# Older tiles ahead of new rows, and three weights transfers behind the fourth tile's rows, in the first rounds of an expert pipeline

## The chip, the cores and the metric

The kernel runs on one core of a Trainium2 chip. The metric is device time in microseconds of one execution; lower is better. TensorE does matmuls and transposes, VectorE, ScalarE and GpSimd work on what it leaves, and SyncE only issues transfers. Each engine takes its own instructions in order and waits for the others by semaphores.

## What is computed

All is float32, on four sequences of 256 tokens of width 256. A bidirectional decaying scan conditions x, an attention block follows (16 heads, 4 key heads), its output is added to x, a second scan conditions the sum, and a mixture of experts closes it. Only the last part matters here:

```python
logits = x @ gate_weight.T
probs = softmax(logits)
w, chosen = top_k(probs, 8)
w = w / w.sum(-1)
for e in range(64):
    gate, up = split(x @ gate_up_weights[e])
    final += combine[:, e] * ((silu(gate) * up) @ down_weights[e])
```

There are 1024 tokens of 256 values, 64 experts, 8 experts per token, and an inner width of 96.

## The kernel before, in words

Each engine has its own program (`block.sync`, `gpsimd`, `scalar`, `vector`, `tensor`), and the order of the work is the order in which these programs are written out.

**Sending.** After attention and routing GpSimd scatters each token's row to a slot of its expert in DRAM (`slot_rows`), eight scatters for each block of 128 tokens. The last two blocks send their 16 scatters at the very end, in an order by expert rank (L613), each pair counted on a semaphore `last_sent[j]`.

**Tiles, groups, rounds.** The expert stage takes tiles of 128 rows: 64 rows of one expert and 64 of the next. 96 tiles are processed (`SEQ`), of which the first 28 and the last 4 are the first rows of each pair of experts and the 64 between are further rows, whose experts are known only at run time. Tiles 0 to 3 are groups of one, later ones groups of two. Rounds are one group each for groups 0 to 3 and two groups (four tiles) each from then on: round 4 is tiles 4 to 7, round 5 tiles 8 to 11.

**A tile's steps.** SyncE loads the 128 rows (`load_rows`, L429, two transfers of 65 KB). Ten row buffers allow it to run ahead; from tile 10 on it waits for the `dest_ready` of the tile ten before. Tile d of the first four also waits for `last_sent[2d]` and `last_sent[2d+1]`. TensorE turns the rows (`turn_rows`, two transposes through L1387), VectorE copies them to SBUF (`copy_turned_rows`, L1306) and reads weight and destination of each row (`find_rows`, L1314). TensorE multiplies by gate and up weights (`gate_up`, L1685), ScalarE takes the silu (`silu`, L833), VectorE multiplies (`weigh`, L1323), TensorE turns the product (`turn_act`, L1387), ScalarE copies it (`copy_turned`), TensorE multiplies by the down weights (`down`, L1706), ScalarE copies the result out (`copy_out`) and GpSimd scatters it to `pair_rows` (L620).

**The software pipeline.** In iteration g TensorE's loop (L1714) does, in this order: dummy matmuls that keep its clock (`keep_clock(IDLE[g])`, L1712, only g = 0 to 3, with 5, 2, 3 and 2 of them), `turn_rows` of round g, `turn_act` of round g-2, `gate_up` of round g-1, `down` of round g-2. VectorE's loop (L1348) copies round g's turned rows and then weighs round g-1; in its first iterations it also makes a table of the further tiles (`tile_table`), whose columns TensorE turns at the end of iteration 5. ScalarE's loop (L882) does `copy_turned` of round g-2, `silu` of round g-1 and `copy_out` of round g-2.

**Weights.** 32 transfers of two experts each fill `wts`. SyncE issues the first 22. Ten are left to ScalarE's queue (`load_two`, L852), since their places are in use until the last rows are sent: three at the end of its iteration 2, behind a wait for `last_sent[7]`, one at the end of iterations 3 to 5, then two at a time. While the expert tiles run, no other transfers but rows, these weights and the outputs' scatters run.

Of the kernel before, what the change touches and what calls it, by code (L numbers as in the profile page):

```python
# [31 lines left out]
def adaln_attn_ffn(nc, x_t, side_t, cond, wu_t, wq_l, wk_l, wv_l, wq_t, wv_t, wgd_l, wo_l, gw_t, experts, out):  # L32
# [14 lines left out]
    TOPK = 8  # L47
# [22 lines left out]
    with ExitStack() as ctx:  # L70
# [7 lines left out]
        def sem(name):  # L78
            return ctx.enter_context(nc.semaphore(name))
# [16 lines left out]
        def tiny(name, shape):  # L96
# [184 lines left out]
        last_sent = [sem(f"last_sent{j}") for j in range(TOPK)]  # L281
# [3 lines left out]
        rows_ld = [sem(f"rows_ld{i}") for i in range(NROW)]  # L285
        gu_copied, dn_copied = sem("gu_copied"), sem("dn_copied")
        xt_done, xt_copied, gu_done, silu_done, act_ready, at_done, at_copied, dn_done, out_copied, dest_ready = (
            sem(n) for n in ("xt_done", "xt_copied", "gu_done", "silu_done", "act_ready", "at_done", "at_copied", "dn_done",
                             "out_copied", "dest_ready"))
# [51 lines left out]
        LAST = (NTB - 2, NTB - 1)  # L341
# [15 lines left out]
        ROUNDS = [[g] for g in range(TOPK // 2)] + [[g, g + 1] for g in range(TOPK // 2, NG, 2)]  # L357
        NR = len(ROUNDS)
        TABLE_AT = 5
        IDLE = (5, 2, 3, 2)  # L360
        AHEAD = 8

        late_two = free_scored + 7

        def two_kept(i):
            return wts[:, 2 * i * EW:2 * (i + 1) * EW].rearrange("p (e n) -> p e n", e=2)

        def two_experts(i):
            return experts[2 * i:2 * i + 2].rearrange("e p n -> p e n")
# [10 lines left out]
        def _(sp):  # L380
# [63 lines left out]
            for d in range(NDBL):  # L444
# [8 lines left out]
                else:  # L453
                    m = j - FIXED
                    if m == 0:
                        sp.wait_ge(rows_ready, 1)
                    if m % AHEAD == 0:
                        _, r16 = nc.values_load_multi_w_load_instructions(
                            t_rows[0:1, 2 * m:2 * (m + AHEAD)], engines=[SP_ENGINE], min_val=0, max_val=NE * CAP - R,
                            skip_runtime_bounds_check_because="each is 0 or an expert's base plus at most its row count less one tile")  # L460
                        for k in range(AHEAD):
                            base_of[m + k] = r16[2 * k:2 * k + 2]
# [163 lines left out]
        def _(act):  # L626
# [194 lines left out]
            def copy_turned(a):  # L821
                n = len(GROUPS[a])
                act.wait_ge(at_done, a + 1)
                if a >= 2:
                    act.wait_ge(dn_done, a - 1)
                copy(aT[a % 2][0:I, 0:n, :], ps[0:I, 4 + a % 2, 0:n * P].rearrange("p (k t) -> p k t", k=n)).then_inc(at_copied, 1)

            def silu(u):
                n = len(GROUPS[u])
                act.wait_ge(gu_done, u + 1)  # L830
                if u >= 1:
                    act.wait_ge(act_ready, u)
                nc.scalar.activation(sact[:, 0:n, :], ps[:, 2 + u % 2, 0:n * I2].rearrange("p (k i) -> p k i", k=n)[:, :, 0:I],  # L833
                                     ACT.Silu).then_inc(silu_done, 1)
# [14 lines left out]
            def load_two(i):  # L849
                if i == free_kept:  # L850
                    act.wait_ge(rows_ready, 1)
                nc.scalar.dma_start(two_kept(i), two_experts(i)).then_inc(wts_ld[2 * i // PER], 16)  # L852
# [3 lines left out]
            def copy_down(g):  # L856
                for d in GROUPS[g]:
# [3 lines left out]
                    if m == 0:  # L861
# [3 lines left out]
                        for i in range(3):  # L865
                            act.wait_ge(scattered[i], 16)
                    if m % AHEAD == 0:
                        _, o8 = nc.values_load_multi_w_load_instructions(
                            t_off[0:1, 1, m:m + AHEAD], engines=[ACT_ENGINE], min_val=0, max_val=(NE - 1) * EW,
                            skip_runtime_bounds_check_because="each is 0 or an expert's number times the width of its weights")  # L870
                        for k in range(AHEAD):
                            dn_off[m + k] = o8[k]
# [8 lines left out]
            next_two = late_two  # L881
            for g in range(NR + 2):  # L882
                us = ROUNDS[g - 1] if 1 <= g <= NR else []
                outs = ROUNDS[g - 2] if g >= 2 else []
                for a in outs:
                    copy_turned(a)
                for u in us:
                    silu(u)
                for a in outs:
                    copy_out(a)  # L890
                for u in us:
                    copy_down(u)
                if g == 2:
                    act.wait_ge(last_sent[TOPK - 1], 16 * len(LAST))
                    for i in range(next_two, next_two + 3):
                        load_two(i)
                    next_two += 3
                elif g > 2:
                    for i in range(next_two, min(next_two + len(outs), FIXED)):
                        load_two(i)  # L900
                        next_two += 1
# [6 lines left out]
        def _(dve):  # L908
# [234 lines left out]
            for u in range(NU):  # L1143
# [40 lines left out]
                if u == NU - 1:  # L1184
                    dve.wait_ge(out_done, NB)
                    xs = xT[:, :, b * T:(b + 1) * T]
                    link(V.tensor_tensor(xs, ps[:, 7, :].rearrange("p (m t) -> p m t", m=CC), xs, ALU.add))
                elif n == KV - 1:
                    dve.wait_ge(out_done, b + 1)
                    xs = xT[:, :, b * T:(b + 1) * T]  # L1190
# [156 lines left out]

            for g in range(NR + 1):  # L1348
                ins_ = ROUNDS[g] if g < NR else []
                for x in ins_:  # L1350
                    copy_turned_rows(x)
                    find_rows(x)
                us = ROUNDS[g - 1] if g else []
                for k in range(max(len(us), len(ins_))):
                    if k < len(us):
                        dve.wait_ge(dest_ready, us[k] + 1)
                        weigh(us[k])
                    if k < len(ins_):
                        copy_gate_up(ins_[k])
                if g == TABLE_AT:  # L1360
                    tile_table(5)
                if g == 0:
                    tile_table(0)
                    tile_table(1)
                elif g == 1:
                    tile_table(2)
                    tile_table(3)
                elif g == 2:
                    tile_table(4)
# [10 lines left out]
        def _(pe):  # L1380
# [253 lines left out]
            def turn_rows(g):  # L1634
                if g >= 2:
                    pe.wait_ge(xt_copied, g - 1)
                for k, d in enumerate(GROUPS[g]):
                    pe.wait_ge(rows_ld[d % NROW], 32 * (d // NROW + 1))
                    for cc in range(CC):
                        ins = T_(ps[:, g % 2, (k * CC + cc) * P:(k * CC + cc + 1) * P], xrow[d % NROW][:, cc * P:(cc + 1) * P])  # L1640
                ins.then_inc(xt_done, 1)
# [47 lines left out]
            def down(a):  # L1689
                pe.wait_ge(at_copied, a + 1)  # L1690
                if a >= 2:
                    pe.wait_ge(out_copied, a - 1)
                for k, d in enumerate(GROUPS[a]):
                    j = SEQ[d]
                    if j >= FIXED:
                        m = j - FIXED
                        pe.wait_ge(dn_copied, m + 1)
                    for h in range(2):
                        if j < FIXED:
                            w = (2 * j + h) * EW + CC * I2  # L1700
                            moving = wts[0:I, w:w + C]
                        elif h == 0:
                            moving = wts[0:I, bass.ds(off_of[m] + CC * I2, C)]
                        else:
                            moving = copy_dn[m % NCOPY][0:I, :]
                        ins = nc.tensor.matmul(ps[h * R:(h + 1) * R, 6 + a % 2, k * C:(k + 1) * C], aT[a % 2][0:I, k, h * R:(h + 1) * R], moving,  # L1706
                                               start=True, stop=True)
                ins.then_inc(dn_done, 1)
# [5 lines left out]
            for g in range(NR + 2):  # L1714
                outs = ROUNDS[g - 2] if g >= 2 else []
                if g < len(IDLE):
                    keep_clock(IDLE[g])
                for x in ROUNDS[g] if g < NR else []:
                    turn_rows(x)
                for a in outs:  # L1720
                    turn_act(a)
                for u in ROUNDS[g - 1] if 1 <= g <= NR else []:
                    gate_up(u)
                for a in outs:
                    down(a)
                if g == TABLE_AT:
                    pe.wait_ge(cols_ready, 1)
                    pe.wait_ge(at_copied, g - 1)
                    for k in range(3):
                        ins = T_(ps[:, 5, k * P:(k + 1) * P], t_cols[:, k:k + 1].to_broadcast([P, P]))  # L1730
                    ins.then_inc(cols_turned, 1)
# [60 lines left out]
```

## Time and profile before

| what | value |
|---|---|
| plain runs, median of 3 | 522.57 us |
| plain runs, lowest to highest | 521.33 to 523.16 us |
| the profiled execution, first to last instruction (its own time as far as it is known) | 576.6 us |
| mean granted TensorE clock in it | 0.947 |
| TensorE busy | 477.4 us (83%) |
| VectorE busy | 342.7 us (59%) |
| ScalarE busy | 305.9 us (53%) |
| GpSimd busy | 212.3 us (37%) |

The profiled execution is 54.0 us longer than the median of the plain runs. All times of rows below are its own, in microseconds from its first instruction. The iterations that the change touches lie between 331 and 360 us. PE is TensorE's matmuls, PEld its weight loads, DVE VectorE, ACT ScalarE, POOL GpSimd, SP SyncE; a q behind an engine is its sequencer, which issues transfers. A matmul is two records in the trace and a transpose one: `turn_rows` of a tile is x2, `gate_up` of a tile x8 and `down` x4.

### The profile page before, as it was taken

To read this page: it belongs to the slowest core of one execution; us is meant where nothing else is said; L and a number is where in the kernel's file an instruction comes from. 1 tells how busy PE (TensorE), PEld (TensorE's weight loads), DVE (VectorE), ACT (ScalarE), POOL (GpSimd) and SP (SyncE) were. 2 spreads that over 40 slices of the span, in tenths; PEclk is the share of its full clock that TensorE was granted. 3 is DMA by queue.
4 is the path that set the end of the run, shared out by engine and by line. 5 is a ranking of instruction groups with operands and counts; after the bars stand their busy time and mean duration, and the time that the engine had idled before them with its cause. 6 is when DMAs were issued, how large, how long until landed. Compare 5 with 4: busy or idle time off the path is not lost. (4 is left out here: it accounts for less than half of the span.)

```text
span 576.6 us, 10371 instructions
## 1 busy us (share of the span) xinstructions
PE 477.4 (83%) x3073; PEld 351.1 (61%) x3073; DVE 342.7 (59%) x1204; ACT 305.9 (53%) x854; POOL 212.3 (37%) x224
## 2 busy tenths in 40 slices
PE   4586999999899899999983766987988888888666
PEld 1366767877787678788653423765665666655322
DVE  4768496596685894795793564544355454553033
ACT  3456787885966887779864201333244343444200
POOL 0344110041114631025584642245444455445600
PEclk9799999999999999999996788999899899899879
DMA  8920862000301102002998739884444444330097
GB/s 283 411 70 19 167 131 74 1 1 0 76 1 54 69 30 73 2 1 74 345 404 291 278 107 298 227 288 129 111 115 115 113 128 127 107 95 13 19 363 304
DMA packets 47318, 79.49 MB, mean 138 GB/s; under 512 B 8266, under 2 KB 31127, under 8 KB 46880
## 3 DMA queue, kind: packets, MB, share of 16 engines
q1 hardware_dynamic: 36864, 55.34, 31.1%
q0 software_dynamic: 7680, 16.93, 8.2%
q10 hardware_dynamic: 2720, 6.55, 3.5%
q8 instruction: 26, 0.43, 0.3%
q14 instruction: 28, 0.23, 0.1%
HBM read 56.54 MB, written 26.44 MB: 144 GB/s over the span
## 5 line engine op out<-in xcount | busy, mean ns | idle before, releaser
L620 POOL DMA_INDIRECT pair_rows<-eout,dest x93 | 91.8, 987 | 99.5 <-ACT eout L634 78.2
L833 ACT ACTIVATE sact<-ps 128x192 f32<-128x192 f32 (+1 forms) x50 | 16.3, 325 | 122.7 <-remote 73.6
L1323 DVE SCALAR_TENSOR_TENSOR aact<-sact,wcol,ps 128x96 f32<-128x96 f32 x96 | 26.0, 311 | 92.6 <-issue 87.1
L1685 PE MATMUL ps<-wts,xg 128*64 (+1 forms) x512 | 71.5, 342 | 3.7 <-DVE copy_gu L1346 2.2
L691 ACT ACTIVATE lg<-lg,mneg 128x128 f32<-128x128 f32 (+1 forms) x128 | 56.4, 443 | 26.1 <-DVE mneg L1029 21.5
L1685 PEld LDWEIGHTS ps<-wts,xg 128*64 128x64 f32 x512 | 53.0, 143 | 16.5 <-issue 9.5
L541 POOL DMA_INDIRECT slot_rows<-rows,pair_slot x48 | 47.9, 998 | 37.2 <-issue 24.1
L1512 PE MATMUL ps<-oT,wo_sb 128*128 128x256 f32 x240 | 54.4, 380 | 0.0
L1706 PE MATMUL ps<-wts,aT 96*64 96x256 f32 (+1 forms) x256 | 49.8, 395 | 4.4 <-issue 3.4
L1512 PEld LDWEIGHTS ps<-oT,wo_sb 128*128 128x128 f32 x240 | 44.6, 190 | 6.2 <-ACT oT L634 0.7
L634 ACT ACTIVATE lg<-lg,rinv 128x128 f32<-128x128 f32 (+1 forms) x128 | 45.9, 448 | 2.5 <-issue 1.7
L1685 PE MATMUL ps<-copy_gu,xg 128*64 128x192 f32 x256 | 46.6, 337 | 0.0
L1029 DVE CUSTOM_DVE_ANT_0 lg<-ps,bm 128x128 f32<-128x128 f32 (+1 forms) x128 | 36.9, 352 | 11.3 <-PE ps L1468 9.5
L1306 DVE COPY xg<-ps 128x512 f32<-128x512 f32 (+1 forms) x50 | 33.2, 664 | 15.4 <-PE ps L1387 8.8
L1387 PE MATMUL ps<-ident,xrow 128*128 128x128 f32 x192 | 31.0, 294 | 12.1 <-DMA xrow<-slot_rows 6.8
L1387 PEld LDWEIGHTS ps<-ident,xrow 128*128 128x128 f32 x192 | 22.3, 149 | 28.6 <-issue 21.2
L1383 PE MATMUL ps<-hh,wqh 128*128 128x256 f32 x128 | 38.1, 298 | 1.6 <-DVE kl L988 1.6
L1706 PE MATMUL ps<-copy_dn,aT 96*64 96x256 f32 x128 | 33.9, 385 | 6.4 <-issue 6.4
L1706 PEld LDWEIGHTS ps<-wts,aT 96*64 96x64 f32 x256 | 27.3, 141 | 15.8 <-issue 4.8
L1384 PE MATMUL ps<-hl,wqh 128*128 128x256 f32 x128 | 36.7, 287 | 0.0
L1385 PE MATMUL ps<-hh,wql 128*128 128x256 f32 x128 | 36.7, 287 | 0.0
L501 POOL TENSOR_TENSOR eukv<-euk,vT 128x512 f32<-128x512 f32 x8 | 10.2, 1273 | 67.1 <-ACT euk L669 50.6
(237 smaller groups left out, 1184.4 us busy)
## 6 DMA issues: line engine op xcount, KB each, us to landing
wts<-in_experts_dram SPq DMA_DIRECT2D x22, 640.0 KB, 8.0
xrow<-slot_rows SPq DMA_DIRECT2D x192, 65.0 KB
pairs<-pair_rows SPq DMA_DIRECT2D x16, 512.0 KB, 11.2
wts<-in_experts_dram ACTq DMA_DIRECT2D x10, 640.0 KB, 6.1
slot_rows<-zero SPq DMA_DIRECT2D x1, 4160.0 KB, 24.2
wT<-in_wq_t_dram SPq DMA_DIRECT2D x4, 512.0 KB, 6.5
wq_raw<-in_wq_l_dram SPq DMA_DIRECT2D x1, 2048.0 KB, 14.6
wo_sb<-in_wo_l_dram SPq DMA_DIRECT2D x1, 2048.0 KB, 20.5
```

The lines of the kernel that those rows point to most:

```text
L541: nc.gpsimd.indirect_dma_start(out=slot_d, out_offset=bass.IndirectOffsetOnAxis(ap=pair_slot[:, t, k:k + 1], axis=0), in_=r[:, k, :], in_o ...
L620: nc.gpsimd.indirect_dma_start(out=pair_d, out_offset=bass.IndirectOffsetOnAxis(ap=dest[:, d:d + 1], axis=0), in_=out_rows(d), in_offset=N ...
L634: copy = lambda o_, i_, s=1.0: nc.scalar.activation(o_, i_, ACT.Copy, scale=s)
L691: ins = nc.scalar.activation(t, t, ACT.Exp, bias=mneg[:, u % 2, c:c + 1], scale=-1.0, accum_out=rsum[:, u % 2, c:c + 1])
L1029: ins = V.tensor_tensor_reduce(t, s, m, 1.0, FLT_BIG, ALU.add, ALU.min, mneg[:, u % 2, c:c + 1])
L1383: nc.tensor.matmul(o_, a[0], b_[0], start=start, stop=False)
L1384: nc.tensor.matmul(o_, a[0], b_[1], start=False, stop=False)
L1385: return nc.tensor.matmul(o_, a[1], b_[0], start=False, stop=stop)
L1387: T_ = lambda o_, i_, n=P: nc.tensor.transpose(o_, i_, ident[0:n, 0:n])
L1512: ins = nc.tensor.matmul(ps[:, 7, m * T:(m + 1) * T], wo_sb[:, n * G + h, m * P:(m + 1) * P], oT[:, h, :], start=(n == 0 and m == 0 and h ...
L1685: ins = nc.tensor.matmul(ps[h * R:(h + 1) * R, 2 + u % 2, k * I2:(k + 1) * I2], xg[u % len(xg)][:, k, cc, h * R:(h + 1) * R], moving, star ...
L1706: ins = nc.tensor.matmul(ps[h * R:(h + 1) * R, 6 + a % 2, k * C:(k + 1) * C], aT[a % 2][0:I, k, h * R:(h + 1) * R], moving, start=True, st ...
```

## The change

The set `OLD_FIRST` holds iterations 1 to 4. In these TensorE does `turn_act`, `gate_up` and `down` of the older rounds first and `turn_rows` of the new round last, and VectorE weighs the older round before it copies the new round's turned rows. The three transfers at the end of ScalarE's iteration 2 stand at the start of its iteration 3, ahead of `copy_turned`, and wait for the landing of tile 3's rows (`rows_ld[3]`) in place of the last pair of scatters. From iteration 5 on nothing is changed.

```diff
--- before.py
+++ after.py
@@ -358,6 +358,7 @@
         NR = len(ROUNDS)
         TABLE_AT = 5
         IDLE = (5, 2, 3, 2)
+        OLD_FIRST = range(1, TOPK // 2 + 1)
         AHEAD = 8
 
         late_two = free_scored + 7
@@ -882,6 +883,11 @@
             for g in range(NR + 2):
                 us = ROUNDS[g - 1] if 1 <= g <= NR else []
                 outs = ROUNDS[g - 2] if g >= 2 else []
+                if g == 3:
+                    act.wait_ge(rows_ld[3], 32)
+                    for i in range(next_two, next_two + 3):
+                        load_two(i)
+                    next_two += 3
                 for a in outs:
                     copy_turned(a)
                 for u in us:
@@ -890,12 +896,7 @@
                     copy_out(a)
                 for u in us:
                     copy_down(u)
-                if g == 2:
-                    act.wait_ge(last_sent[TOPK - 1], 16 * len(LAST))
-                    for i in range(next_two, next_two + 3):
-                        load_two(i)
-                    next_two += 3
-                elif g > 2:
+                if g > 2:
                     for i in range(next_two, min(next_two + len(outs), FIXED)):
                         load_two(i)
                         next_two += 1
@@ -1347,12 +1348,16 @@
 
             for g in range(NR + 1):
                 ins_ = ROUNDS[g] if g < NR else []
+                us = ROUNDS[g - 1] if g else []
+                if g in OLD_FIRST:
+                    for u in us:
+                        dve.wait_ge(dest_ready, u + 1)
+                        weigh(u)
                 for x in ins_:
                     copy_turned_rows(x)
                     find_rows(x)
-                us = ROUNDS[g - 1] if g else []
                 for k in range(max(len(us), len(ins_))):
-                    if k < len(us):
+                    if k < len(us) and g not in OLD_FIRST:
                         dve.wait_ge(dest_ready, us[k] + 1)
                         weigh(us[k])
                     if k < len(ins_):
@@ -1715,7 +1720,8 @@
                 outs = ROUNDS[g - 2] if g >= 2 else []
                 if g < len(IDLE):
                     keep_clock(IDLE[g])
-                for x in ROUNDS[g] if g < NR else []:
+                xs = ROUNDS[g] if g < NR else []
+                for x in xs if g not in OLD_FIRST else []:
                     turn_rows(x)
                 for a in outs:
                     turn_act(a)
@@ -1723,6 +1729,8 @@
                     gate_up(u)
                 for a in outs:
                     down(a)
+                for x in xs if g in OLD_FIRST else []:
+                    turn_rows(x)
                 if g == TABLE_AT:
                     pe.wait_ge(cols_ready, 1)
                     pe.wait_ge(at_copied, g - 1)
```

## Rows read from the trace of the kernel before

**Rows 1.** The page: busy time of each engine, and one kind of weights transfer.

```profile
PE 477.4 (83%) x3073; PEld 351.1 (61%) x3073; DVE 342.7 (59%) x1204; ACT 305.9 (53%) x854; POOL 212.3 (37%) x224
...
wts<-in_experts_dram ACTq DMA_DIRECT2D x10, 640.0 KB, 6.1
```

**Rows 2.** Stretches: us, busy per engine (instructions), granted clock, DMA share, GB/s.

```profile
342.00:347.50 5.50, 4.41 (x15) 2.25 (x16) 4.67 (x12) 1.16 (x4) 0.40 (x1) 0.50 0.47 94
347.50:354.00 6.50, 4.16 (x24) 2.21 (x22) 2.13 (x10) 0.91 (x3) 1.80 (x2) 0.89 0.97 340
354.00:360.00 6.00, 3.38 (x23) 2.07 (x24) 2.45 (x11) 0.91 (x3) 0.98 (x1) 0.93 1.09 298
...
403.00:500.00 97.00, 82.60 (x710) 58.85 (x711) 47.33 (x210) 38.17 (x112) 47.20 (x48) 0.96 0.42 116
```

**Rows 3.** TensorE's waits, 360 to 540 us: total us, times, longest.

```profile
PE ps L1706 <- issue: 9.8, 16, 1.1
...
PE ps L1387 <- DMA xrow<-slot_rows: 1.4, 1, 1.4
```

**Rows 4.** Timeline of TensorE: start, us, line, tiles, count, [idle before <-what ended it].

```profile
334.31 0.87 PE L1685 MATMUL ps<-wts,xg 128*64 128x192 f32 x8
...
339.05 0.41 PE L1387 MATMUL ps<-ident,xrow 128*128 128x128 f32 x2 [1.09 <-DMA xrow<-slot_rows]
...
343.47 1.55 PE L1685 MATMUL ps<-wts,xg 128*64 128x192 f32 x8
344.81 1.07 PE L1706 MATMUL ps<-wts,aT 96*64 96x256 f32 x4
345.81 3.49 PE L1712 MATMUL ps<-x2tm,ident 128*128 128x512 f32 x4
349.13 0.38 PE L1387 MATMUL ps<-ident,xrow 128*128 128x128 f32 x2
349.35 0.27 PE L1387 MATMUL ps<-ident,aact 128*96 128x128 f32 x1
...
354.05 0.44 PE L1387 MATMUL ps<-ident,xrow 128*128 128x128 f32 x2 [2.38 <-DMA xrow<-slot_rows]
354.32 0.27 PE L1387 MATMUL ps<-ident,aact 128*96 128x128 f32 x1
...
355.76 0.86 PE L1387 MATMUL ps<-ident,xrow 128*128 128x128 f32 x4
...
359.61 0.69 PE L1387 MATMUL ps<-ident,xrow 128*128 128x128 f32 x2 [1.37 <-DMA xrow<-slot_rows]
...
360.44 3.83 PE L1685 MATMUL ps<-wts,xg 128*64 128x192 f32 x32
364.10 0.60 PE L1706 MATMUL ps<-wts,aT 96*64 96x256 f32 x4
```

**Rows 5.** Timeline of SyncE's queue, three short stretches: loads of the expert rows.

```profile
336.64 0.47 SPq L429 DMA_DIRECT2D xrow<-slot_rows  x1
...
341.63 1.10 SPq L429 DMA_DIRECT2D xrow<-slot_rows  x2
...
351.24 1.87 SPq L429 DMA_DIRECT2D xrow<-slot_rows  x3
```

**Rows 6.** Timeline of ScalarE and of the transfers that it issues.

```profile
342.37 0.25 ACT L833 ACTIVATE sact<-ps 128x96 f32<-128x96 f32 x1 [20.15 <-remote]
...
345.93 1.50 ACTq L852 DMA_DIRECT2D wts<-in_experts_dram  x3
...
350.91 0.37 ACTq L852 DMA_DIRECT2D wts<-in_experts_dram  x1
...
355.88 0.42 ACTq L852 DMA_DIRECT2D wts<-in_experts_dram  x1
```

**Rows 7.** Timeline of VectorE: one copy of turned rows.

```profile
345.47 0.42 DVE L1306 COPY xg<-ps 128x256 f32<-128x256 f32 x1
```

**Rows 8.** The stretch 359 to 360 us; columns as in rows 2.

```profile
359.00:360.00 1.00, 0.39 (x2) 0.40 (x3) 0.00 (x0) 0.00 (x0) 0.00 (x0) 0.56 1.12 277
```

## The prediction, made before the changed kernel was run

> **What bounds the kernel now.** I began with the page. TensorE is busy for 477.4 of 576.6 us [rows 1], so it is the first suspect everywhere, but a mean over stages says little about thirty microseconds of one of them. The second view is the table of stretches [rows 2]. From 403 to 500 us TensorE is busy 82.6 of 97 us and the DMA engines 0.42: this is the steady pipeline, bound by TensorE's own stream. From 342 to 360 us, where the edited rounds run, it is busy only 4.4 of 5.5, 4.2 of 6.5 and 3.4 of 6 us, while the DMA share goes from 0.47 to 0.97 and then 1.09. So the first rounds are bound by something that arrives, and the rest by TensorE. The waits of TensorE from 360 us to the end of the experts confirm the second half: one wait of 1.4 us for rows among all of them (it spills over from 359.6) [rows 3]. A microsecond won or lost before round 5's matmuls should therefore go one to one into the time; one won anywhere earlier counts only if round 5 starts earlier.
>
> The third view is TensorE's timeline [rows 4]. Round 5 turns tiles 8 to 11 first; its last two transposes start at 359.61 after a wait of 1.37 us for the DMA of rows, and only then come turn_act(3), 32 records of gate_up at 360.44 and down(3) at 364.10. Round 4 has the same shape: the last transposes, tile 7's, start at 354.05 after 2.38 us of waiting for rows; the older steps run from 354.32 to 355.76. Round 3 does not wait for rows: tile 3 is turned at 349.13, right behind a keep_clock(2) that took from 345.81 on at the low clock.
>
> Why do rows come late? SyncE issues each tile's two loads back to back, 0.62 us apiece (three in 1.87 us) [rows 5]. Counting from tile 3 at 341.63, tile 11's two are the last two of the three that begin at 351.24, so they are issued by 353.11. Tile 2 shows what a load costs when little else moves: issue over at 336.64 + 0.47 = 337.11, rows used at 339.05 on ending a DMA wait, 1.94 us [rows 4, 5]. At that price tile 11 would be here at 353.11 + 1.94 = 355.05; it was used at 359.61. The 4.56 us between are contention: the three late weights transfers go out at 345.93 [rows 6], two more at 350.91 and 355.88, 640 KB each, five of the ten that ScalarE issues [rows 1], and the engines are full from 347.5 [rows 2].
>
> **The change, part by part.**
> The wait of the three weights transfers. Today it is for the last scatter, after which tile 3's loads are issued too (341.63). Tomorrow it is for tile 3's landing: 341.63 + 1.10 + 1.94 = 344.7 [rows 4, 5]. But ScalarE gets there only behind copy_out(0), at 345.93 [rows 6]. The new wait is thus met 1.2 us before it is reached: cost 0. It stands ahead of copy_turned(1) of round 3, as the old one did at the end of round 2; what is queued behind it on ScalarE is copy_turned(1), silu(2), copy_out(1) and the fourth weights transfer, and behind these TensorE's down(1) and, new, turn_rows(3), which now follows down(1). If ScalarE came early, this would be a real stall: bounds 0 and, if ScalarE were ready right after the last scatter at 341.63, 344.7 - 341.6 = 3.1 us. I take 0, since the row nearest is ScalarE's own. Nothing else on a DMA queue moves: the three issues, 1.50 us together, stay between copy_out(0) and copy_turned(1).
>
> Round 1. TensorE does gate_up(0) before turning tile 1, and VectorE does weigh(0) before it copies tile 1. In the trace silu(0) starts only at 342.37 although gate_up(0)'s records end at 335.2, an idle stretch put down to "remote" [rows 4, 6]. If that lag stays, VectorE's copy of tile 1 moves behind weigh(0), to about 343.1, and takes 0.42 us as another 128x256 copy does [rows 7]: 343.5, against gate_up(1) at 343.47 now: no gain, no loss. The two table steps of this round follow that copy in either version, now later; they have until the table's transposes, behind down(3) at 364.10.
>
> Round 2. down(0) no longer stands behind tile 2's transposes, which had arrived anyway. 0.
>
> Round 3. The older steps of tile 1 and 2 run ahead of tile 3's transposes. Both follow keep_clock(2), which holds TensorE until 349.13 [rows 4]. Tile 3 has been there since 344.7, so nothing is waited for by going either way: the fourth weights transfer goes out some 0.3 to 0.5 us later, since tile 2's transposes now precede keep_clock(2). It is queued behind the first three, which at the 340 GB/s of the stretch [rows 2], 0.34 MB a microsecond, need 1.92 / 0.34 = 5.6 us from about 347.5, to 353: its own issue at 350.91 is not what sets its start. 0.
>
> Round 4. Here the order acts. turn_act(2), gate_up(3) and down(2), 354.32 to 355.76 = 1.44 us, leave the place behind tile 7's arrival and fill the 2.38 us gap before it [rows 4]. Then tile 7 is turned at the same 354.05 and TensorE goes on to round 5 1.44 us sooner, at 354.3. Round 5, outside the edited range, still turns tiles 8 to 11 first, and tile 11 comes at 359.61. The 1.44 us are added to the gaps that end there. Late next: tile 11. Gain 0 unless tile 11 moves. Its loads hang on SyncE's stream, which in this stretch waits for neither TensorE nor VectorE (0.62 us after 0.62 us), and on the same five transfers. The fifth now goes out about 2 us sooner (down(2) ends near 353.4 instead of 355.8), but it is served behind the fourth; at 0.34 MB a microsecond four transfers take until about 355 alone and near 358 with the rows between them, so its earlier issue brings between 0 and -1 us of contention to tile 11. I take 0.
>
> **Sum.** 0 + 0 + 0 + 0 - 0: the profiled execution would stay at 576.6 us. That execution is 54.0 us above the plain median of 522.57 (521.33 to 523.16), so its microseconds are not to be taken at face value one by one; I carry the difference, zero, over to the plain runs: 522.6. A measurement can tell about 0.3%, 1.6 us, from no change.
>
> **Rivals.**
> Faster: TensorE's order is what delays the rows' users, and in plain runs tile 11 isn't late. For it: those runs are 54 us shorter, so the contention may be less. With tile 11 in time, the 1.44 us of round 4 and as much of round 3 (the same steps for the tile before, from 349.35 on, at the same clock) come out of the path: 2.9 us, 519.7. The most that can go is the whole contention on tile 11, 4.56 us: 518.0. Against it: even with free DMA engines SyncE's stream holds tile 11 until 355.05, after round 4's work at 354.3.
>
> Slower, one mechanism: the clock. Between 354.3 and 359.6 TensorE keeps only transposes once the 1.44 us of matmuls have moved out. Now it is granted 0.56 of its clock at 359 to 360 us [rows 8], the lower level, 1.2 GHz, after it was nearly idle, and part of gate_up(4, 5) runs at it: 3.66 us from 360.44 to 364.10. If the clock is at the low level for the whole of round 5's older steps, a tile's gate_up takes 344.81 - 343.47 = 1.34 us [rows 4], four of them 5.4, 1.7 more than now, and down(3) 1.00 instead of 0.6: together +2.2 us, 524.8. It decides if the clock falls before 359 and isn't back before 364. The Trainium skill, "TensorE: Matmul & The Clock Gate", section "HAM oscillation — how this bites in real kernels", says that work in short bursts between waits for DMA is throttled again at each wait, which speaks against emptying this stretch; the trace agrees, with 0.56 at 359. By that page alone the result would be this rival's.
>
> The second way to a loss has the same size: in a plain run without the 7 us lag ScalarE is at the transfers right after the last scatter, and the new wait holds them, and all behind them, up to 3.1 us; DMA engines that stood at 0.47 then stay idle longer and tile 11 comes later by part of it. I count it in the range and in the slower chance.
>
> The change may also do nothing that it says: the new wait is met before it is reached. That is part of my forecast.
>
> **Chances.** No change 0.40; the faster rival 0.34, since gaps on three engines shrink in these rounds and only one arrival keeps them from counting; clock 0.12 and held-back transfers 0.14, slower 0.26 in all. The range runs from a little beyond the faster rival, 519.0, to a little beyond the slower one, 525.2.
>
> **What would show it.** After: tile 7's transposes still end a wait for rows near 354, now with turn_act(2), gate_up(3) and down(2) before them; tile 11's still end a wait near 359.6 and the gap before is longer by 1.4 us; ScalarE's three transfers go out within 0.5 us of 345.9; copy_turned(1) isn't held. Wrong if round 5's gate_up starts over 1.5 us earlier (or later) relative to the last scatter, if ScalarE sits before the transfers waiting for rows, or if gate_up(4, 5) takes 5 us.

## The result, and the profile after

The changed kernel is slower: 528.24 us median (524.33 to 531.02, 17 runs) against 523.89 us (520.45 to 528.09, 17 runs) of the kernel before on the same chips. The ratio is 1.0070, with a 95% interval of 1.0044 to 1.0095, so the 0.7% (3.7 us) is clear of noise; the two medians lie 4.35 us apart, and I go by the ratio. I had forecast no change.

The first reading is a correction of my own reference. The changed kernel was profiled in an execution of 527.56 us, span 525.8. The profile on which the prediction rests had a span of 576.6. A second profile of the unchanged kernel (run `base_again`) has a span of 524.3, in an execution of 526.11 us, the slowest of its twelve (the fastest took 521.50), so it too is no average execution. The stretches of that second profile, with the columns of rows 2, at the same distances from the last scatter of rows as rows 2:

```profile
331.50:337.00 5.50, 1.43 (x4) 0.36 (x2) 2.44 (x9) 0.00 (x0) 1.00 (x1) 0.94 0.85 271
337.00:343.50 6.50, 5.58 (x28) 3.64 (x30) 2.21 (x10) 1.13 (x4) 0.99 (x1) 0.53 1.02 287
343.50:349.50 6.00, 5.40 (x57) 3.88 (x53) 3.76 (x18) 1.57 (x6) 0.98 (x1) 1.00 0.97 296
...
392.50:489.50 97.00, 96.61 (x970) 74.34 (x969) 64.81 (x270) 59.71 (x164) 65.62 (x67) 1.00 0.45 131
```

and of the changed kernel:

```profile
331.00:336.50 5.50, 3.15 (x18) 1.33 (x17) 2.77 (x10) 0.64 (x3) 1.00 (x1) 0.94 0.59 143
336.50:343.00 6.50, 4.67 (x22) 2.39 (x20) 1.99 (x9) 1.07 (x4) 1.98 (x2) 0.50 1.06 352
343.00:349.00 6.00, 2.70 (x8) 1.16 (x8) 2.13 (x10) 0.00 (x0) 0.00 (x0) 0.50 1.07 331
...
392.00:489.00 97.00, 96.61 (x974) 74.67 (x972) 65.83 (x275) 60.34 (x165) 64.02 (x65) 1.00 0.47 132
```

Set beside [rows 2], the last line of each matters most. In the steady part TensorE is busy 96.6 of 97 us in both, not 82.6. The first profile was of an execution in which much else waited, and the wait structure that I read from it (ScalarE idle until 342.37, [rows 6]) was its own. In the other lines the two kernels part: in the third stretch TensorE is busy 5.40 of 6 us before and 2.70 after, at a granted clock of 1.00 before and 0.50 after, with the DMA engines full in both (0.97, 1.07). The changed kernel is still waiting for rows there.

The pages, sections 1 and 5: the changed kernel's line of busy times, and its wait of TensorE for rows over the whole span.

```profile
PE 459.3 (87%) x3073; PEld 344.4 (65%) x3073; DVE 345.9 (66%) x1204; ACT 310.1 (59%) x854; POOL 213.3 (41%) x224
...
L1392 PE MATMUL ps<-ident,xrow 128*128 128x128 f32 x192 | 30.3, 295 | 5.8 <-DMA xrow<-slot_rows 5.8
```

To compare stages I count from the start of the last of the scatters: 328.63 in `base_again`, 328.14 in the changed kernel. (Over all profiles it lies between 325.37 and 331.06, and for one kernel run twice, `order_only` and `order_again`, at 325.77 and 327.97, so a part of what executions differ by comes before the stage that the change touches.) In the timelines the columns are start, busy time, engine, line, operation and, in brackets, the idle time before it and what ended it; ACTq is ScalarE's issuing of DMAs. GpSimd's timeline of the kernel before, second profile:

```profile
328.63 0.96 POOL L613 DMA_INDIRECT slot_rows<-rows,pair_slot  x1 [0.31 <-issue]
```

its ScalarE's:

```profile
325.60 0.25 ACT L833 ACTIVATE sact<-ps 128x96 f32<-128x96 f32 x1 [14.44 <-PE ps L1685]
...
331.07 0.38 ACT L634 ACTIVATE eout_first<-ps 128x256 f32<-128x256 f32 x1 [0.18 <-PE ps L1706]
331.12 1.49 ACTq L852 DMA_DIRECT2D wts<-in_experts_dram  x3
338.84 0.27 ACT L634 ACTIVATE aT<-ps 96x128 f32<-96x128 f32 x1 [7.38 <-PE ps L1387]
...
341.19 0.38 ACTq L852 DMA_DIRECT2D wts<-in_experts_dram  x1
...
344.53 0.37 ACTq L852 DMA_DIRECT2D wts<-in_experts_dram  x1
```

and its TensorE's:

```profile
324.68 0.87 PE L1685 MATMUL ps<-wts,xg 128*64 128x192 f32 x8
...
337.93 0.66 PE L1387 MATMUL ps<-ident,xrow 128*128 128x128 f32 x2 [4.99 <-DMA xrow<-slot_rows]
...
345.88 0.44 PE L1387 MATMUL ps<-ident,xrow 128*128 128x128 f32 x2 [0.60 <-DMA xrow<-slot_rows]
...
346.36 2.82 PE L1685 MATMUL ps<-wts,xg 128*64 128x192 f32 x32
...
352.51 0.95 PE L1387 MATMUL ps<-ident,xrow 128*128 128x128 f32 x4 [1.99 <-DMA xrow<-slot_rows]
...
354.17 4.10 PE L1685 MATMUL ps<-wts,xg 128*64 128x192 f32 x32
```

The same three of the changed kernel, GpSimd's:

```profile
328.14 0.96 POOL L614 DMA_INDIRECT slot_rows<-rows,pair_slot  x1 [0.30 <-issue]
```

ScalarE's:

```profile
330.15 0.39 ACT L635 ACTIVATE eout_first<-ps 128x256 f32<-128x256 f32 x1 [0.18 <-PE ps L1711]
333.38 1.70 ACTq L853 DMA_DIRECT2D wts<-in_experts_dram  x3
335.13 0.27 ACT L635 ACTIVATE aT<-ps 96x128 f32<-96x128 f32 x1 [4.59 <-issue]
...
336.28 0.39 ACTq L853 DMA_DIRECT2D wts<-in_experts_dram  x1
...
339.82 0.38 ACTq L853 DMA_DIRECT2D wts<-in_experts_dram  x1
```

TensorE's:

```profile
336.17 0.69 PE L1392 MATMUL ps<-ident,xrow 128*128 128x128 f32 x2
...
343.00 0.69 PE L1392 MATMUL ps<-ident,xrow 128*128 128x128 f32 x2 [0.93 <-DMA xrow<-slot_rows]
344.82 0.66 PE L1392 MATMUL ps<-ident,xrow 128*128 128x128 f32 x2 [1.13 <-DMA xrow<-slot_rows]
...
349.36 0.69 PE L1392 MATMUL ps<-ident,xrow 128*128 128x128 f32 x2 [0.43 <-DMA xrow<-slot_rows]
...
350.19 4.14 PE L1690 MATMUL ps<-wts,xg 128*64 128x192 f32 x32
...
357.01 2.82 PE L1690 MATMUL ps<-wts,xg 128*64 128x192 f32 x32
```

What is to be seen, in microseconds after that scatter:

| | before (`base_again`) | changed |
|---|---|---|
| ScalarE's first three weights transfers | 2.5 | 5.2 |
| copy_turned(1) | 10.2 | 7.0 |
| fourth transfer | 12.6 | 8.1 |
| fifth transfer | 15.9 | 11.7 |
| tile 3 turned | 9.3 | 8.0 |
| tile 11 turned (last transposes of round 5) | 17.3 | 21.2 |
| duration of gate_up(4, 5), 32 records | 2.82 us | 4.14 us |
| duration of gate_up(6, 7), 32 records | 4.10 us | 2.82 us |

ScalarE is done with copy_out(0) at 330.15 + 0.39 = 330.54 and stands idle until 333.38: the new wait holds it for 2.8 us, and copy_turned(1) behind it has 4.59 us of idle time before it. Tile 3 does come earlier. Then both later weights transfers go out over 4 us sooner than before, and tile 11 is turned 4.0 us later and still ends a wait for its rows, whose loads were issued at the same distance in both. By the start of round 7 (tile 16) the difference is down to 2.1 us, 33.4 against 31.3: in round 6 it is the kernel before that waits 1.99 us for rows (at 352.51) and then runs its 32 records of gate_up at the low clock.

### The profile page after: what moved, and what is told of

The parts are those of the page before. It is cut to its first block and busy times, and to the rows that moved or that the text cites. A ratio compares the mean times of both kernels' runs of the same rounds, so it can differ in the third digit from the quotient of the medians.

```text
span 525.8 us, 10369 instructions
## 1 busy us (share of the span) xinstructions
PE 459.3 (87%) x3073; PEld 344.4 (65%) x3073; DVE 345.9 (66%) x1204; ACT 310.1 (59%) x854; POOL 213.3 (41%) x224
## 5 line engine op out<-in xcount | busy, mean ns | idle before, releaser
L1690 PE MATMUL ps<-wts,xg 128*64 (+1 forms) x512 | 70.3, 339 | 1.5 <-DVE xg L1307 1.5
L1690 PEld LDWEIGHTS ps<-wts,xg 128*64 128x64 f32 x512 | 52.2, 141 | 14.5 <-issue 5.8
L1711 PE MATMUL ps<-wts,aT 96*64 96x256 f32 (+1 forms) x256 | 46.7, 385 | 3.2 <-ACT aT L635 3.2
L1690 PE MATMUL ps<-copy_gu,xg 128*64 128x192 f32 x256 | 45.0, 329 | 0.0
L635 ACT ACTIVATE eout<-ps 128x512 f32<-128x512 f32 (+1 forms) x47 | 27.8, 594 | 24.6 <-PE ps L1711 13.5
L502 POOL TENSOR_TENSOR eukv<-euk,vT 128x512 f32<-128x512 f32 x8 | 10.2, 1273 | 66.3 <-ACT euk L670 50.7
L508 POOL TENSOR_TENSOR df<-df,euk 128x512 f32<-128x512 f32 x7 | 8.9, 1275 | 67.4 <-DVE df L971 67.3
```

What stands on the lines that cost most here:

```text
L635: copy = lambda o_, i_, s=1.0: nc.scalar.activation(o_, i_, ACT.Copy, scale=s)
L1690: ins = nc.tensor.matmul(ps[h * R:(h + 1) * R, 2 + u % 2, k * I2:(k + 1) * I2], xg[u % len(xg)][:, k, cc, h * R:(h + 1) * R], moving, star ...
```

## The experiments

All ratios are to the unchanged kernel on the same chip, each from 5 rounds (11 or 12 timed executions, 6 for `late_all_before`); the change's own is that of the 17 executions above. "Tile 11" and "tile 16" are the starts of their transposes after the last scatter's issue, in the one profiled execution of each run; they tell when TensorE came to these tiles, which is not always when the rows came.

| run | order | first three wait for | fourth, fifth at the end of iteration | ratio (95%) | tile 11 | tile 16 |
|---|---|---|---|---|---|---|
| base_again | old | scatters | 3, 4 | 1.0013 (0.9983-1.0042) | 17.3 | 31.3 |
| the change | new | tile 3 | 3, 4 | 1.0070 (1.0044-1.0095) | 21.2 | 33.4 |
| wait_only | old | tile 3 | 3, 4 | 1.0019 (0.9987-1.0051) | 19.6 | 30.0 |
| order_only | new | scatters | 3, 4 | 1.0050 (1.0017-1.0083) | 19.1 | 31.0 |
| order_again | new | scatters | 3, 4 | 1.0042 (1.0015-1.0069) | 19.3 | 32.3 |
| behind_copy | new | tile 3, end of 3 | 3, 4 | 1.0071 (1.0034-1.0107) | 20.7 | 33.8 |
| order_pinned | new | scatters | 4, 5 | 0.9989 (0.9960-1.0018) | 17.7 | 31.0 |
| order_fifth_late | new | scatters | 3, 5 | 1.0000 (0.9972-1.0028) | 17.2 | 27.7 |
| change_pinned | new | tile 3 | 4, 5 | 1.0041 (1.0009-1.0073) | 20.3 | 32.8 |
| change_fifth_late | new | tile 3 | 3, 5 | 1.0017 (0.9988-1.0046) | 20.0 | 32.4 |
| fourth_early | old | scatters | 2, 4 | 1.0004 (0.9975-1.0033) | 20.3 | 30.7 |
| before_fifth_late | old | scatters | 3, 5 | 0.9997 (0.9964-1.0031) | 17.6 | 28.0 |
| late_all_before | old | all ten in 5 to 8 | - | 1.0111 (1.0064-1.0157) | 15.5 | 27.7 |
| late_all_order | new | all ten in 5 to 8 | - | 1.0050 (1.0016-1.0085) | 15.5 | 28.7 |
| change_keep | new, dummies | tile 3 | 3, 4 | 1.0061 (1.0035-1.0087) | 21.4 | 31.9 |
| pinned_keep | new, dummies | scatters | 4, 5 | 0.9999 (0.9970-1.0027) | 19.4 | 29.8 |
| before_keep | old, dummies | scatters | 3, 4 | 0.9992 (0.9960-1.0024) | 20.0 | 30.4 |

### The two parts apart

My theory A was that the new wait costs, by holding ScalarE; B that the order costs.

`base_again` is the kernel before, with no edit.

> The kernel before, unchanged, for a second profile of it: the first one's execution was 54 us longer than its plain runs. All theories: ratio 1.00, within 0.3%. If the 7 us lag between gate_up(0) and silu(0) belonged to that execution alone, silu(0) starts here within 1 us of gate_up(0)'s end, ScalarE is at the three weights transfers when the last scatters land, and the span is near 522 us.

Measured 1.0013. In the second profile silu(0), at 325.60, follows gate_up(0), whose records end at 324.68 + 0.87 = 325.55, and ScalarE sends the three transfers 2.5 us after the last scatter is issued. The 7 us lag of [rows 4, 6] was that one execution's.

`wait_only` takes the change's wait and leaves the order:

```diff
+                if g == 3:
+                    act.wait_ge(rows_ld[3], 32)
+                    for i in range(next_two, next_two + 3):
+                        load_two(i)
+                    next_two += 3
                 for a in outs:
                     copy_turned(a)
...
-                if g == 2:
-                    act.wait_ge(last_sent[TOPK - 1], 16 * len(LAST))
...
```

> Only the three transfers are moved; the order of TensorE's and VectorE's steps is that of before. Theory A (the new wait holds ScalarE, and with it copy_turned(1), down(1) and the next weights transfers): slower by 2 to 4 us, 0.4 to 0.8%, and ScalarE idle for about 3 us or more before the transfers. Theory B (the order costs, since tile 3's and later rows are turned behind older steps and the clock falls): within 0.3% of before.

1.0019 (0.9987 to 1.0051): inside B's answer and below A's 2 to 4 us, though the interval still reaches A's lower end.

`order_only` takes the order and leaves the transfers as before:

```diff
+        OLD_FIRST = range(1, TOPK // 2 + 1)
```

(with its uses in VectorE's and TensorE's loops; ScalarE's loop is that of before).

> Only the order of TensorE's and VectorE's steps is changed; the three transfers wait for the last scatter at the end of iteration 2 as before. Theory A: within 0.3% of before, or faster by up to 1.5 us. Theory B: slower by 3 to 4 us, as the whole change. Theory C (the two parts cost only together, since down(1) now stands ahead of turn_rows(3) and is held by ScalarE): order alone 0, wait alone 0 to 1 us.

1.0050, 1.0017 to 1.0083: the order costs, a little less than B said, and A doesn't hold as the only cause. Its profile happened to be of the fastest of its twelve executions (521.9 us), so I repeated the kernel in the last group:

> The order alone, the same kernel as order_only, for a narrower interval and a second profile (the first was of its fastest run). All theories that hold the order to cost: 1.003 to 1.007, mean granted clock about 0.955 against 0.961 of before. If the first result was drawn high: within 0.2% of 1.

1.0042, 1.0015 to 1.0069. The order's cost stands.

`behind_copy` is the whole change with the three transfers moved behind copy_out(1):

```diff
-                if g == 3:
-                    act.wait_ge(rows_ld[3], 32)
...
                 for a in outs:
                     copy_turned(a)
...
                 for u in us:
                     copy_down(u)
+                if g == 3:
+                    act.wait_ge(rows_ld[3], 32)
...
```

> The whole change, but the three transfers stand at the end of ScalarE's iteration 3, behind copy_turned(1), silu(2) and copy_out(1), so that the wait for tile 3's rows holds nothing but transfers. Theory A in its form that the held copies cost: within 0.3% of before. Theory D (what costs is that the weights start later, and so still contend with tiles 8 to 11): as slow as the whole change or slower, 3 to 5 us, since they start later still.

1.0071: not holding the copies gained nothing, which is the answer of B and of D. The run doesn't price the copies by themselves, though. The three transfers begin 5.5 us after the last scatter, 0.3 us later than in the change, but the fifth, whose turn comes sooner with nothing held, goes out at 8.9 us instead of 11.7, and what the copies win can be lost there.

### Which transfers

In `order_only` nothing holds ScalarE. TensorE gives it round 1's work before tile 3's rows are in, it copies that out, and then sends the fourth transfer; then, behind copy_out(2), the fifth. ScalarE's transfers in that run, whose last scatter is issued at 325.77:

```profile
328.23 1.49 ACTq L853 DMA_DIRECT2D wts<-in_experts_dram  x3
...
331.22 0.37 ACTq L853 DMA_DIRECT2D wts<-in_experts_dram  x1
...
339.01 0.37 ACTq L853 DMA_DIRECT2D wts<-in_experts_dram  x1
```

The fourth is at 5.5 us and the fifth at 13.2, where the kernel before has 12.6 and 15.9. That made theory E: the order costs because it sends weights ahead of rows.

`order_pinned`, new order, both held back:

```diff
+            LATE = {2: 3, 4: 1, 5: 2, 6: 2, 7: 2}
...
+                for i in range(next_two, next_two + LATE.get(g, 0)):
```

> The new order of steps with the first three transfers as before (last scatter, end of iteration 2), and the fourth and fifth held back by an iteration each: the fourth at the end of iteration 4, the fifth at the end of 5, so that the fourth goes out about 13 us after the last scatter's issue, as in the kernel before, and not at 5.4 as with the new order alone. Theory E (the new order costs because it lets ScalarE send the fourth and fifth transfers before the rows of tiles 8 to 11 are in): tile 11 is turned at 17 to 18 us after the last scatter's issue, against 19.1 with the order alone, and the ratio goes from 1.005 to within 0.3% of 1. Theory B (the order itself or the clock costs): still 1.004 to 1.006.

0.9989, tile 11 at 17.7: as expected, although the 32 records of gate_up(4, 5) ran at the low clock throughout (5.35 us). One thing in the profiles doesn't follow: tile 16 is at 31.0 us here and in `order_only`, so the 0.6% between the two is not to be seen by the start of round 7.

`fourth_early`, old order, `LATE = {2: 4, 4: 1, 5: 1, 6: 2, 7: 2}`:

> The kernel before with only the fourth transfer moved, to right behind the first three at the end of iteration 2. Theory E: slower by 0.3 to 0.6%, tile 11 turned about 2 us later than the 17.3 of before. Theory B: within 0.3% of before.

1.0004, a miss, and an instructive one. TensorE's timeline, last scatter at 325.37:

```profile
341.39 0.69 PE L1384 MATMUL ps<-ident,xrow 128*128 128x128 f32 x2 [0.80 <-DMA xrow<-slot_rows]
...
344.56 1.47 PE L1384 MATMUL ps<-ident,xrow 128*128 128x128 f32 x8
...
346.07 2.82 PE L1682 MATMUL ps<-wts,xg 128*64 128x192 f32 x32
```

Tile 11 is turned late, at 20.3 us, but not because its rows are late: tiles 8 to 11 follow the older steps of round 4 without a wait. It is round 4 that waited, for tile 7, until 341.39 (16.0 us). The fifth transfer goes out at 19.3, since in the old order it stands behind work that waits for round 4's rows. Round 6 doesn't wait for rows either, but nor does it in the changed kernel. What differs from there is that round 5's gate_up runs at the full clock here (2.82 us, not 4.14), and tile 16 is at 30.7 us, not 33.4. So the start of tile 11's transposes alone is not the measure.

`order_fifth_late`, new order, fourth where `order_only` has it, fifth at the end of iteration 5, `LATE = {2: 3, 3: 1, 5: 2, 6: 2, 7: 2}`, tests the fifth alone (theory G):

> The new order, first three transfers as before, the fourth at the end of iteration 3 (about 5.4 us after the last scatter's issue), the fifth moved from the end of iteration 4 to the end of 5. Theory G (what costs is five transfers ahead of tile 11's rows; four do not): ratio within 0.3% of 1, tile 11 turned by 18.5 us. If the fourth matters in the new order: still 1.003 to 1.006.

1.0000, against 1.0050 and 1.0042 with the fifth at the end of iteration 4. Its profile, TensorE's timeline:

```profile
343.73 2.21 PE L1389 MATMUL ps<-ident,xrow 128*128 128x128 f32 x10 [0.20 <-DMA xrow<-slot_rows]
...
345.97 2.82 PE L1687 MATMUL ps<-wts,xg 128*64 128x192 f32 x32
...
349.54 1.04 PE L1389 MATMUL ps<-ident,xrow 128*128 128x128 f32 x8
```

Tile 11 is the end of the row at 343.73 (17.2 us after the scatter at 328.30), and round 5's gate_up takes 2.82 us at the full clock. `order_again` and this run differ in the place of one transfer in ScalarE's loop, and by 0.4%; `order_only` and `order_pinned` differ by 0.6% with two transfers moved. Within the intervals, of about 0.3% to either side of each ratio, the fifth transfer is the whole cost of the order. By which path its earlier issue costs is less clear: in this profile tile 16 is at 27.7 us, over 3 us ahead of all runs that send the fifth in iteration 4 with the same order, and from there to the last instruction it takes 167.5 us (355.96 to 523.5) where `base_again` takes 164.4.

`change_fifth_late` and `change_pinned` do the same in the whole change, `LATE = {3: 1, 5: 2, ...}` and `{4: 1, 5: 2, ...}`:

> The whole change with only the fifth transfer moved to the end of iteration 5. Theory G: 1.000 to 1.004, tile 11 turned near 19.5 us instead of 21.2. If the fourth matters too: 1.004 to 1.007.

> The whole change with its wait for tile 3's rows, but the fourth transfer at the end of iteration 4 and the fifth at the end of 5. Theory G: no more than the hold of ScalarE is left, which alone measured 1.0019: ratio 0.999 to 1.003. If hold and order cost together by another way: 1.005 to 1.008.

1.0017 and 1.0041. The first is as expected: moving the fifth takes the whole change from 1.0070 to 1.0017. The second is a miss (0.999 to 1.003 was forecast), and its interval, from 1.0009, doesn't hold 1. Both leave something, more than the same schedules without the new wait (1.0000 and 0.9989). I put that down to the hold: 0.2% in `wait_only`, 0.2% and 0.5% here, each with an interval of some 0.3% to either side. I take it as 0.2 to 0.5%, about 1 to 2.5 us, and its size as open, down to nothing, since only `change_pinned` tells it from 0.

### Can the transfers go later still?

`before_fifth_late`, the old order with the fifth moved:

> The kernel before with only the fifth transfer moved, from the end of iteration 4 to the end of 5, behind tile 11's rows. Theory E: the 2.0 us for which tile 14's rows are awaited in iteration 6 go, tile 11 is turned at 16 to 17 us, and the time falls by 1 to 2 us, 0.996 to 0.998. If contention only moves: within 0.3%.

0.9997, the answer of contention that only moves. Tile 16 is turned at 28.0 us instead of 31.3 in the profiles, and the time is the same; from tile 16 to the last instruction it takes 166.1 us instead of 164.4, with a wait of 1.03 us for rows in round 8, so about half of the gain is given back there. `late_all_before` and `late_all_order` send all ten in iterations 5 to 8, `LATE = {5: 2, 6: 3, 7: 3, 8: 2}`:

> The kernel before with all ten late transfers sent in iterations 5 to 8 (2, 3, 3 and 2), when tile 11's rows are there. Theory E in full (contention of late weights with the rows is what bounds the first rounds): tile 3 is in by 5 to 6 us after the last scatter's issue, tile 11 is turned at 15 to 16 instead of 17.3, and the time falls by 1 to 4 us. If the contention only moves to tiles 12 to 23: within 0.3% of before. Theory B says nothing of it: 0.

> The same, in the new order of steps. Theory E: like the run with the order of before, within 0.3% of it, since tile 11's arrival bounds both. Theory B: slower than that run by 0.4 to 0.6%.

1.0111 and 1.0050: slower than before, which no theory had forecast, though tile 11 is there at 15.5 in both. TensorE's timeline of `late_all_before`, last scatter at 328.95:

```profile
351.13 2.82 PE L1682 MATMUL ps<-wts,xg 128*64 128x192 f32 x32
...
356.63 0.41 PE L1384 MATMUL ps<-ident,xrow 128*128 128x128 f32 x2 [0.95 <-DMA xrow<-slot_rows]
357.47 0.44 PE L1384 MATMUL ps<-ident,xrow 128*128 128x128 f32 x2 [0.43 <-DMA xrow<-slot_rows]
358.14 0.86 PE L1384 MATMUL ps<-ident,xrow 128*128 128x128 f32 x4 [0.23 <-DMA xrow<-slot_rows]
...
367.50 0.69 PE L1384 MATMUL ps<-ident,xrow 128*128 128x128 f32 x2 [2.41 <-DMA xrow<-slot_rows]
```

Rounds 5 and 6 are early, and rounds 7 and 8 wait for rows: 0.95, 0.43, 0.23 and 2.41 us. The five transfers that no longer compete with tiles 3 to 11 compete with 16 to 23. The two differ by 0.6%, though I had expected them to be equal if arrival alone bounds them. Their intervals overlap, and the first ratio is of 6 executions; whether the old order really loses here, and why, is open.

### The clock

The changed kernel is granted half the clock from 7.7 to 24.8 us after the last scatter, `base_again` from 7.7 to 14.5 and again from 24.8 to 28.2, in round 6, where its 32 records of gate_up take 4.10 us. So it is 17.1 us of low clock against 10.2, and the 1.3 us that the change loses in round 5's gate_up the profiled execution before loses in round 6's. My slower rival had the first half of this. Over all timed executions the mean granted clock is 0.954 for the change, 0.954 and 0.955 for the order alone, and 0.962 for `base_again`. To see its price, three kernels got dummy matmuls in iteration 5:

```diff
+                if g == TABLE_AT:
+                    keep_clock(3)
                 for x in xs if g not in OLD_FIRST else []:
                     turn_rows(x)
+                    if g == TABLE_AT and x == xs[0]:
+                        keep_clock(1)
```

> The whole change, with dummy matmuls in iteration 5: three before tiles 8 and 9 are turned, one before 10 and 11. Theory F (part of the cost is TensorE's clock: with the older steps moved away, iteration 4's end and iteration 5's beginning hold only transposes, and the matmuls of iteration 5 run at the low level): the 32 records of iteration 5's gate_up, 3.8 us from first to last start with the whole change, take 2.5 as in the order of before, the step from tile 11's to tile 12's transposes falls from 5.7 to 4.0 us, and the ratio from 1.007 to 1.002 to 1.004. Theory E alone (only tile 11's arrival counts): unchanged at 1.007.

> The new order with the fourth and fifth transfers pinned late, and the same dummy matmuls. Theory F: the step from tile 11 to tile 12 falls from 6.9 to 4.0 us, tile 16 is turned near 28 us after the last scatter's issue, and the ratio is 0.994, faster than both kernels. Theory E alone: as without the dummies, 0.999.

> A control: the kernel before with the same dummy matmuls. Its iteration 5 has the full clock already (2.5 us for the 32 records). Theory F: within 0.3% of before. If dummies in this place help or cost by themselves, this run shows it.

1.0061, 0.9999 and 0.9992. The clock does come back in time; `change_keep`, TensorE's timeline:

```profile
340.86 4.41 PE L1717 MATMUL ps<-x2tm,ident 128*128 128x512 f32 x6
345.11 0.60 PE L1392 MATMUL ps<-ident,xrow 128*128 128x128 f32 x4
...
347.33 2.82 PE L1690 MATMUL ps<-wts,xg 128*64 128x192 f32 x32
...
350.90 1.04 PE L1392 MATMUL ps<-ident,xrow 128*128 128x128 f32 x8
```

These 32 records of gate_up(4, 5) take 2.82 us instead of 4.14, and the step from tile 11 to tile 12 falls from 5.7 to 4.1 us, as theory F said, but the dummies themselves run at the low level (six records in 4.41 us) and hold tiles 8 and 9. The mean granted clock rises from 0.954 to 0.959, and the ratio goes only from 1.0070 to 1.0061, well within the intervals. With the transfers pinned, dummies gain nothing (0.9989 and 0.9999), where theory F had 0.994. So the low clock is real, 1.3 us in round 5's gate_up, and stands where TensorE waited; `order_pinned` has it in full and measures 0.9989, so the low clock in that round is not by itself the cost, and taking it away in this manner is not shown to pay.

## Why the prediction was wrong

**What bounds it.** That rows' arrival bounds the first rounds and TensorE the rest was right, and is sharper in a clean profile (96.6 of 97 us). "One to one into the time" was too strong: `before_fifth_late` starts round 7 3.3 us sooner in the profile and gains nothing, since later rounds give part of it back.

**The wait.** "The new wait is thus met 1.2 us before it is reached: cost 0" failed. It held because ScalarE was at 345.93, behind a silu(0) that started 7 us late in that execution. In the changed kernel's profile ScalarE is held 2.8 us, close to the upper bound that I gave, 3.1 us, and `wait_only` prices it at 0.2%, not distinguished from 0. The bound was right, the point in it wrong, since I let one row of an execution 54 us too long choose it.

**Rounds 1 to 3.** No cost of their own is shown: `order_fifth_late`, which has all of the new order, measures 1.0000. But the forecast that the fourth transfer goes out 0.3 to 0.5 us later was wrong in its sign. It goes out 4.4 us sooner in the changed kernel and 7.1 with the order alone, since it hangs on round 1's older steps, which no longer stand behind the wait for tile 3's rows (4.99 us in `base_again`); the first profile, in which tile 3 was there in time, had no such wait. `order_fifth_late` has this fourth transfer and shows that it costs nothing.

**Round 4, the step that failed.** I wrote that the 1.44 us of older steps only fill a gap, which holds, and that the fifth transfer's going out about 2 us sooner "brings between 0 and -1 us of contention". It goes out 4.2 us sooner in the changed kernel and 2.7 with the order alone, and this is the term that was mis-sized: 1.0050 and 1.0042 with it, 1.0000 without, so about 0.45% or 2.4 us where I had allowed up to 1 us and taken 0. I had reasoned that it queues behind the fourth anyway, with the three transfers beginning 6.8 us after the last scatter (345.93, scatter at 339.13). In `base_again` they begin after 2.5 us and in the changed kernel after 5.2, the fourth and fifth follow at 8.1 and 11.7, and so five transfers of 640 KB are issued before tile 11's loads, at about 12.7 us, where the kernel before has four. With the order alone the fifth goes out at 13.2, just behind those loads and 6 us before tile 11 is used. The Trainium skill, "DMA: Bandwidth & Descriptors", section "Issuing engines are not separate DMA queues", says that transfers started by ScalarE and SyncE run on the same DMA engines and interleave; the traces agree: tile 11's loads are issued at the same distance and used 4.0 us later. That the fifth transfer costs is shown by moving it; that it costs through these rows is argued from the profiles, and `fourth_early` and `order_pinned` show that the time doesn't simply follow tile 11 or tile 16.

**The sum.** 0 against 3.7 us measured, 0.7%: about 0.45% from the fifth transfer, and 0.2 to 0.5% from the hold; these add up within their intervals, so no third cause is needed, though none is excluded.

**The rivals.** The faster one failed on the row that I had named against it: tile 11 bounds. The clock came true in the trace, with 4.14 us for gate_up(4, 5) where I had computed 5.4, but restoring it took no measurable time off. (Its sum was off by a little: 1.7 and 0.4 are 2.1 us, not 2.2.) The second way to a loss, the held transfers of a run without the lag, is what happened to the wait, and I had given it 0.14. The earlier fifth transfer, the larger part, was in none of the rivals.

**What I said would show it.** Tile 11's wait, later by over 1.5 us, and ScalarE sitting before the transfers were both on the list of what would prove me wrong, and both are there.

## What to carry to other kernels

When steps move ahead on one engine, list the transfers that its consumers issue behind them: an engine that finishes sooner sends its next transfers sooner, and these may compete with the data on which everything waits; here the gap that is filled was worth nothing and the earlier transfer cost 0.45%. A hold of three transfers does little if the next go free: with the fifth moved the whole change went from 1.0070 to 1.0017. And a profiled execution that lies 10% above the plain runs tells durations of instructions, not who waits for whom: profile the kernel again before the sum, or spread the chances over what its lags would hide.

## What the runs showed that I had not expected

The start of tile 11 doesn't rank the kernels: with it at 20.3 us after the scatter `fourth_early` measures 1.0004, with it at 21.2 the change measures 1.0070, and with it at 15.5 `late_all_before` measures 1.0111. One transfer can be moved behind round 5 at no cost; moving all ten behind it costs, with waits for rows in rounds 7 and 8. What sets the limit between the two is not shown. And executions of one kernel differ by 1 to 2%, and the longer ones are granted less clock: over the 17 executions of the changed kernel time and mean granted clock have a correlation of -0.72. Profiles of single executions therefore rank these kernels wrongly: order_only's profiled execution was 521.9 us, base_again's 526.1.
